# A written list of all 4928 steps with their banks, and the mix's tanh kept in PSUM

## The reference, cut to what matters

```python
x = x + gated_linear_attention(layernorm(x))   # block a: in-projection, causal conv of 4 taps, silu,
                                                # 32 heads: att = qk * decay * level weight, y = att @ v,
                                                # y * silu(z), rms norm, out-projection
x = x + ffn(layernorm(x))                       # 16-head softmax attention, then 8 experts (relu), top 2 of 8
x = x + mix(layernorm(x))                       # see below
x = x + ffn(layernorm(x))                       # the same ffn weights again

def mix(x):                                     # SHIFTS = (-32, -16, -4, -1, 1, 4, 16, 32)
    v = x @ value_W.T
    stacked = [v] + [roll(v, -s, axis=1) for s in SHIFTS]      # 9 of them
    gates = sigmoid(x @ gate_W.T)                              # 9 x 128 columns
    return layernorm(sum(stacked * gates))
```

## Time and profile before

| what | value |
|---|---|
| median of 3 runs | 2105.55 us |
| the profiled execution, its own time | 2103.15 us |
| its span, first to last instruction | 2101.4 us |
| PE busy | 1921.0 us, 91% |
| DVE busy | 1738.5 us, 83% |
| ACT busy | 1488.0 us, 71% |
| POOL busy | 775.6 us, 37% |
| mean granted TensorE clock | 0.966 |

### The profile page before, as it was taken

One profiled execution on the slowest core, in us unless ns is written; L12 is line 12 of the kernel. 1 busy time (PEld: TensorE's weight loads), 2 busy tenths in 40 slices (PEclk: granted clock), 3 DMA queues, 4 the chain that ended last, 5 costly groups with the idle time before them and its releaser, 6 DMA issues.

```text
span 2101.4 us, 48245 instructions
## 1 busy us (share of the span) xinstructions
PE 1921.0 (91%) x16928; PEld 1491.0 (71%) x16928; DVE 1738.5 (83%) x4463; ACT 1488.0 (71%) x3207; POOL 775.6 (37%) x1139
## 2 busy tenths in 40 slices
PE   4779899999999999999999999999999999997757
PEld 3556677777877777786877778786777778774545
DVE  5776988989898988989898998989898898865643
ACT  4566768778686868778686877868686877855332
POOL 5313353525243343525244352424334352423120
PEclk8889999999999999999999999999999999998867
DMA  5021232211222222211222222121222221112110
GB/s 162 12 63 12 60 67 60 65 41 46 50 59 67 62 67 63 56 35 51 59 60 67 62 64 56 45 44 54 67 60 67 62 63 38 50 53 71 27 56 6
DMA packets 224576, 117.14 MB, mean 56 GB/s; under 512 B 124360, under 2 KB 210512, under 8 KB 219216
## 3 DMA queue, kind: packets, MB, share of 16 engines
...
## 4 chain that ended last, share of the span: by engine, by line
PE 64%; DVE 23%; ACT 4%; issue 4%; SPq 2%; POOL 2%; DMA 1%; DVEq 0%; ACTq 0%; POOLq 0%
DVE nmax L1295 6%; PE psA L862 6%; PE psB L724 6%; DVE work L1220 5%; PE psB L874 5%; PE psA L874 5%; PE psA L699 5%; PE psB L803 3%; PE psB L862 3%; PE psA L630 3%; PE psB L699 2%; PE psA L803 2%; DVE att L1247 2%; DVE hid L1408 2%; PE psA L788 2%
## 5 line engine op out<-in xcount | busy, mean ns | idle before, releaser
L1247 DVE TENSOR_TENSOR att<-att,QK 128x1024 f32<-128x1024 f32 x192 | 251.2, 1341 | 15.2 <-ACT att L1003 15.1
L1529 POOL TENSOR_TENSOR own<-X,ccoef 128x512 f32<-128x512 f32 x128 | 160.2, 1257 | 206.7 <-PE psA L699 97.1
L1437 POOL TENSOR_SCALAR var_eps<-lnmv 128x2 f32<-128x2 f32 x128 | 40.4, 316 | 524.0 <-DVE lnmv L1110 521.3
L1220 DVE SCALAR_TENSOR_TENSOR work<-psA,c_conv_w,work 128x255 f32<-128x255 f32 (+2 forms) x450 | 195.4, 474 | 11.8 <-ACT work L961 11.8
L630 PE MATMUL psA<-xnT_a,c_w_in 128*128 128x256 f32 x608 | 177.9, 397 | 17.8 <-DVE hid L1220 8.7
L1072 ACT ACTIVATE hid<-psA,c_b 128x256 f32<-128x256 f32 x295 | 135.8, 485 | 79.4 <-PE psA L862 79.2
L1295 DVE TENSOR_REDUCE nmax<-psB 128x2 f32<-128x512 f32 x288 | 186.6, 680 | 1.1 <-PE psB L765 1.1
L862 PE MATMUL psA<-x1T,c_w 128*128 128x256 f32 x608 | 178.9, 394 | 1.5 <-DVE nmax L1295 1.3
L1049 ACT ACTIVATE pt<-psB 128x512 f32<-128x512 f32 x256 | 147.4, 614 | 31.5 <-PE psB L789 31.4
L1295 DVE TENSOR_REDUCE nmax<-psA 128x2 f32<-128x512 f32 x224 | 149.8, 681 | 15.1 <-PE psA L765 14.9
L1220 DVE SCALAR_TENSOR_TENSOR work<-psB,c_conv_w,work 128x255 f32<-128x255 f32 (+1 forms) x360 | 159.0, 474 | 2.7 <-ACT work L961 2.1
...
## 6 DMA issues: line engine op xcount, KB each, us to landing
...
k_max<-qk_scr SPq DMA_DIRECT2D x128, 64.0 KB, 2.0
q_max<-qk_scr SPq DMA_DIRECT2D x128, 64.0 KB, 2.0
...
```

The costliest lines, as they stand in the source:

```text
L1220: m = e.scalar_tensor_tensor(out=cv[:, back:], in0=t[:, 0:T - back], scalar=conv_w[:, c, tap:tap + 1], in1=cv[:, back:], op0=ALU.mult, op1 ...
L1247: e.tensor_tensor(att[:, :, :], att[:, :, :], bc(QK[:, kq, :], 1, HG), ALU.mult).then_inc(att_done, 1)
L1529: e.tensor_tensor(own_b[k % 2][:, :].rearrange("p (h c) -> p h c", c=HD), X[:, tt, h0 * HD:(h0 + HG) * HD].rearrange("p (h c) -> p h c", c ...
```

## The change

`PERIOD`, `START` and the unrolling go; the steps of all sequences stand in `ORDER`, 4928 words such as `smax0.1.0@2514` (step 1 of `smax`, first ffn, sequence 0, banks 2, 5, 1, 4). A step may stand at another place and have other banks for each sequence. The sequences are as deep in each other as before. The list needs 78 table loads where there were 66.

The tanh of the mix goes to the other half of its own PSUM bank, DVE reads it from there, and DVE, not ACT, frees the bank. ACT no longer waits for the products. `mix_prod` goes, `tanh_done` comes.

Some waits are written out that the fixed turn had given: outp for gated, the first up for tail 4, gated and own for two steps instead of one, rowmax for the maximum of before. POOL's wait after the square root is moved to the next one's start.

```diff
-PERIOD = """
-up0.2+3@03 relu0.3+3 silu0.1+1 load_x0.0+0 ocopy1.3+4 up0.3+3@51 lvl0.0+1 lvl0.1+1 down0.2+3@7 experts1.3+5
...
+ORDER = """
+load_x0.0.0 gates0.0.0 load_x0.0.1 gates0.6.0 gates0.1.0@0 lvl0.0.0 gates0.2.0@12 gates0.3.0 gates0.4.0@3 cpart0.0.0 conv0.2.0@45 gates0.5.0
...
 def order():
-    period = list(hop_words(PERIOD))
...
+    for hop, _ in hop_words(ORDER):
+        what, _, n, step = hop
...
-    banks = dict(hop_banks(PERIOD))
+    banks = dict(hop_words(ORDER))
...
+        first_up = {}
+        for hop in hops:
+            if hop[0] == "up":
+                first_up.setdefault(hop[1:3], hop)
...
@@ PE
+                    e.wait_ge(*empty(("sum", 0, n, NU // 2 * (k + 1) - 1)))
...
+                    if hop == first_up[lay, n]:
+                        e.wait_ge(*empty(("tail", lay, n, 4)))
@@ ACT
                     if n:
-                        e.wait_ge(mix_prod, NG * n)
+                        e.wait_ge(*empty(("mix", lay, n - 1, NG + 1)))
...
                 elif what == "mix" and 2 <= k < NG + 2:
                     t, b, u = bank(hop)
-                    j = k - 2
-                    e.wait_ge(filled[b], u + 1)
-                    if j >= 2:
-                        e.wait_ge(mix_prod, NG * n + j - 1)
-                    e.activation(hid_b[0][j % 2][:, 0, :], t[:, 0:T], ACT.Tanh, scale=0.5).then_inc(drained[b], 1)
+                    e.wait_ge(filled[b], u + 1)
+                    e.activation(t[:, T:2 * T], t[:, 0:T], ACT.Tanh, scale=0.5).then_inc(tanh_done, 1)
@@ DVE
                     if tt == 0:
+                        e.wait_ge(*empty(("zgate", 0, n, 2 * hg), 1))
                         e.wait_ge(*empty(("zgate", 0, n, 2 * hg + 1), 1))
...
                     i = k // 2
+                    if nth[hop]:
+                        e.wait_ge(nmax_ready, nth[hop])
...
-                    th, prod = hid_b[0][j % 2][:, 0, :], (mix_acc[:, :] if j == 0 else hid_b[0][j % 2][:, 1, :])
+                    t, b, u = bank(hop)
+                    prod = mix_acc[:, :] if j == 0 else hid_b[0][j % 2][:, 1, :]
...
-                    e.wait_ge(*empty(hop))
-                    e.scalar_tensor_tensor(out=prod, in0=th, scalar=1.0, in1=v_ext[:, MAXSH + shift:MAXSH + shift + T],
-                                           op0=ALU.add, op1=ALU.mult).then_inc(mix_prod, 1)
+                    e.wait_ge(tanh_done, NG * n + j + 1)
+                    e.scalar_tensor_tensor(out=prod, in0=t[:, T:2 * T], scalar=1.0, in1=v_ext[:, MAXSH + shift:MAXSH + shift + T],
+                                           op0=ALU.add, op1=ALU.mult).then_inc(drained[b], 1)
@@ POOL
                     e.wait_ge(var_ready, roots[hop])
+                    if roots[hop] > 1:
+                        e.wait_ge(rstd_ready, roots[hop] - 1)
...
-                    e.wait_ge(rstd_ready, roots[hop])
...
-                    e.wait_ge(mix_prod, NG * n + j + 1)
-                    if j > 1:
+                    e.wait_ge(*empty(hop))
+                    if j == 1:
+                        e.wait_ge(*empty(("mix", lay, n, 2)))
+                    else:
                         e.wait_ge(mix_sum, (NG - 1) * n + j - 1)
```

More of the change, by code:

```diff
@@ L129 @@
[L129 to L138, removed]
@@ new lines @@
+smax0.1.12@7310 up1.0.10@42 mix1.8.11@7 mix1.9.11@3 conv0.8.13@15 silu0.7.13 tap0.8.13 taps0.8.13 zgate0.7.13@06 mix1.10.11@4 xt0.6.13@2
+experts1.0.10@7 load_x0.0.15 zact0.7.13 zgate0.1.13@37 smax0.2.12@0631 zact0.1.13 rowmax0.2.12 xt0.5.13@7 xcopy0.6.13 up1.1.10@52 silu0.8.13
+experts1.1.10@4 relu1.1.10 lvl0.7.13 xcopy0.5.13 mix1.11.11@0 rowmax0.3.12 down1.0.10@5 weigh0.0.13@62 smax0.3.12@3701 up1.2.10@46 wexp0.0.13
+wexp0.3.13 relu1.2.10 mix1.12.11 down1.1.10@2 weigh0.3.13@37 up1.3.10@01 maxt0.0.12@3 gates0.1.14@7 fn1.0.11 xt0.7.13@4 acc1.0.10 own0.0.13
@@ L158 @@
+experts1.3.15
 """
@@ L165, in hop_words @@
     for word in text.split():
-        name, rest = word.split(".")
-        step, n = rest.split("@")[0].split("+")
-        yield name[:-1], int(name[-1]), int(step), int(n)
-def hop_banks(text):
-    for word in text.split():
-        name, rest = word.split(".")
-        if "@" in rest:
-            yield (name[:-1], int(name[-1]), int(rest.split("+")[0])), tuple(int(b) for b in rest.split("@")[1])
-def order():
-    period = list(hop_words(PERIOD))
-    runs = [(what, lay, n, step) for what, lay, step, n in hop_words(START) if n < BATCH]
-    ahead = set(runs)
-    for turn in range(BATCH + max(lag for _, _, _, lag in period)):
-        runs += [(what, lay, turn - lag, step) for what, lay, step, lag in period
-                 if 0 <= turn - lag < BATCH and (what, lay, turn - lag, step) not in ahead]
+        name, step, rest = word.split(".")
+        n, _, used = rest.partition("@")
+        yield (name[:-1], int(name[-1]), int(n), int(step)), tuple(int(b) for b in used)
+def order():
     hops, held = [], "exp_set"
-    for what, lay, n, step in runs:
+    for hop, _ in hop_words(ORDER):
+        what, _, n, step = hop
         needed = ("silu_set" if what in SILU_SET else "exp_set" if step in EXP_SET.get(what, ()) else held)
@@ L190, in order @@
             held = needed
-        hops.append((what, lay, n, step))
+        hops.append(hop)
     return hops
@@ L197, in build @@
     hops = order()
-    banks = dict(hop_banks(PERIOD))
+    banks = dict(hop_words(ORDER))
     bank_at, nth, uses, seen_hops = {}, {}, [0] * 8, {}
     for hop in hops:
-        for j, b in enumerate(banks.get((hop[0], hop[1], hop[3]), ())):
+        for j, b in enumerate(banks.get(hop, ())):
             bank_at[hop, j] = (b, uses[b])
```

403 lines of the change are left out of this document (381 added, 22 removed).

## The result

The changed kernel takes 2115.68 us (median of 5, 2112.27 to 2118.46), the kernel before 2105.71 in the same comparison: a ratio of 1.0045, 95% interval 1.0030 to 1.0059. It is slower by 10 us; forecast were 2091 us and 0.7% faster. The profiled execution took 2114.81 us with a span of 2113.0, at a mean granted clock of 0.967 (0.966 before).

What follows compares the result with a forecast made beforehand. Each turn was taken as a DVE-bound stretch of 33 us and a PE-bound one of 86. The terms -7 - 5 - 8 + 3 + 0 + 2 summed to -15 us, giving 2091 us, 0.7% faster; forecast's range 2080 to 2099, overall 2068 to 2116.

Steps and rivals of the forecast that it cites:

- parts 1 and 2: New banks for the mix and `up` (-7 us), and for `sum` (-5 us, bounds 0 to -6.6).
- the named waits: PE's waits once a turn: `up` for `rowmax` (0.77 us), last mix gate for a tanh (0.7), `sum` for `gated` (0.44).
- part 1: Banks of the mix and `up`: 0.5 us saved a turn, 14 turns, -7 us (bounds 0 and -21).
- the DVE-bound stretch: Some 33 us of each turn, from `acc` of expert 7 to the transpose of the maxima, with DVE as the bound.
- Rival D: Order also removes 8 us of stalls hidden in busy PE, both ends give 20: -35 us, 2070 us; chance 0.15.
- signs of being wrong: Prediction called wrong if PE's idle time in the middle does not fall, or the ends change by over 20 us.
- part 3: Head and end of the run: steps move by a few us at most, -8 us (0 to -20).
- part 4: Twelve more table loads on ACT, 1.283 us each, mostly covered by ACT's idle time: +3 us (0 to +15.4).
- part 5: Mix gates' tanh and DVE's product through PSUM: 0 us, bounds 6 us to both sides.
- part 6: Gate banks held until DVE has multiplied, behind up to four maxima: +2 us (0 to +38).
- Rival B: PE stands at the next user of a gate's bank, 2.4 us a turn: +17 in all, 2122 us; chance 0.22.
- part 7: The other waits repeat what the order gives anyway, and POOL covers its moved one: 0 us.

Runs made afterwards that it cites:

- k5: Changed kernel's code with the old order and banks planned anew from the trace of the kernel before: 2085.55 us, ratio 0.9904 to the kernel before.
- k16: Changed kernel's order with banks planned anew and 68 table loads instead of 78: 2105.49 us, ratio 1.0001 to the kernel before.
- k14: Changed kernel with `mix` 12 ahead of the first weight exponential in five turns, 68 table loads instead of 78: 2105.57 us, ratio 1.0011 to the kernel before.
- k1: Changed kernel's code, tanh in PSUM included, with the order and banks of the kernel before: 2172.14 us, ratio 1.0314 to the kernel before.
- k4: Order and banks of the kernel before, tanh into SBUF; only the change's added waits are left: 2107.25 us, ratio 1.0010 to the kernel before.
- k8: Changed kernel's order and code, banks planned anew from its own trace: 2107.09 us, ratio 1.0031 to the kernel before.
- k11: Old order with planned banks, `xcopy` 1 placed some nine ACT steps later, as in the new list: 2081.92 us, ratio 0.9893 to the kernel before.
- k12: Old order with planned banks, two PE steps (`zgate` 5, `xt` 2) earlier in sequences 3 to 12: 2115.02 us, ratio 1.0059 to the kernel before.
- k13: Old order with planned banks, four DVE steps reordered (products 2, 6; gated products 0, 4), sequences 3 to 12: 2110.66 us, ratio 1.0034 to the kernel before.
- k7: Changed kernel with its own banks, ten bank-emptying steps moved back close behind their matmuls, sequences 2 to 13: 2174.23 us, ratio 1.0352 to the kernel before.

## Why the prediction was wrong

*Banks of the mix, `up` and `sum` (parts 1 and 2, -12).* The mechanism was right: the named waits went, and from step to step PE lost 23.8 us less. The old order with new banks has a turn of 118.54 us where 118.5 was forecast. That agreement is luck in part: the forecast was for the new order and three waits, and k5 gives another bank to 2679 of the 3840 uses.

*The step that failed* is in part 1. It held that the DVE-bound stretch can only shrink, by 0.5 us a turn, since "the order on DVE there is what it was"; the order of the steps that feed DVE got no term. The stretch grew by 1.22 us a turn. Rival D was turned down with "PE's steps are moved by a few us and the rest is as it was". But 463 of the 2288 steps with PE work, 377 of 1808 of ACT and 202 of 1553 of DVE stand outside the common order (for each engine's own steps, the longest sequence that both lists share). In the stretch DVE's work is the same, and it waits for tanh, `smax` and taps that come later. The missing term is about +20 us (k16 against k5). It shows in that stretch, 34.78 us for 32.72, and on PE inside steps, 1523.6 us for 1494.9. It is a reading mistake too: I looked for stalls as idle time of PE and named what hides in busy PE only as a gain to be had. The prediction's signs of being wrong had the same blind spot. PE's idle time in the middle did fall, and the ends changed by less than 20 us; what did not come were the turn of 118.5 us (120.95) and DVE over 94% busy in the stretch (92%).

*Head and end (part 3, -8).* Up to `outp` of sequence 2: 295.1 to 297.5 us; behind `outp` 13: 488.6 to 482.0. Together -4.2, right in sign and half in size. PE's wait for q_max at the end stays, 9.8 us. With planned banks the old end is as short (480.7), so banks alone can give that gain.

*Twelve table loads (part 4, +3).* Ten cost 7 us, so some +8: within the bounds, mis-sized. Why ACT's idle time covered no more of them was not looked into. The section on the change took the pairs for the work of a `zact`; five of the six were of no use, and leaving them out is free. The Trainium skill's rule (ScalarE: Activation LUTs, "Table sets: the hidden batching unit") is to batch by set; read as all loads paid, at the trace's 1283 ns, it gives 12.8 for the ten, and k14 bears out a little over half of it. My 3 for the twelve, 2.5 for ten, was about as far off on the other side.

*Gates through PSUM (part 5, 0 within 6).* Product 418 to 415 ns, tanh 392 to 368 ns: 144 x 27 = 3.9 us of engine time; measured 8 (3 to 12) on the new list and 1.5, within noise, on the old order with new banks. The Trainium skill's rule for DVE (Perfetto Trace Analysis, "Optimizing Scalar/DVE Operations", more access time on PSUM) stays unseen in the product. The same sentence gives ScalarE less on PSUM, 51 for 93 ns; the trace has the sign and 24 of these 42 ns.

*Banks held longer (part 6, +2, bounds 0 to 38).* In the changed kernel 1.1 us of waits for the product in the middle: right. Rival B named the mechanism, and k1 shows it at 66 us, the clock's part included, beyond the bound, since PE waits for a gate's bank four times a turn where I had counted one. B foretold the sign of the result for the wrong reason: in the new list it hardly happens.

*The other waits (part 7, 0).* The added ones cost 0.1% in k4: right for these.

The account, in per cent of the kernel before: new banks under the old order, with the tanh edit, give -0.96 (k5); the new order puts 0.97 on top (k16), its ten table loads and its own banks another 0.44 together; that makes the +0.45 measured. These are differences along one chain of runs and add up by construction; the loads (k14, 0.34) and the banks (k8, 0.14) taken singly come to 0.48, which is a check. What stays open is which moves make the 0.97. ACT's largest (`xcopy` 1, nine steps later) costs nothing (k11). Moves of two steps of PE and four of DVE cost 1.3 to 1.8% each on the old order, but by waits that the changed kernel does not have (k12, k13), and part of that may be the clock. That fuller banks are the cause inside steps, and not just their company, isn't shown: k7, meant to show it, changed the table loads too, and had fewer banks in use and more time inside steps.
